# Turning the rounded tokens for the gate and up products by DMA transposes instead of TensorE and ScalarE, in a one-core vision-transformer layer

## The reference

```python
def _act_fake_quant(x, clip_factor):
    scale = jax.nn.sigmoid(clip_factor) * jnp.max(jnp.abs(x)) / QMAX
    return jnp.clip(_ste_round(x / scale), -QMAX - 1.0, QMAX) * scale

xq = _act_fake_quant(x, clip_x[0])                                # (32, 256, 256)
gate = jnp.einsum('bsh,ih->bsi', xq, _weight_fake_quant(w_gate))  # 704 columns
up = jnp.einsum('bsh,ih->bsi', xq, _weight_fake_quant(w_up))
h = _act_fake_quant(jax.nn.silu(gate) * up, clip_down[0])
return jnp.einsum('bsi,hi->bsh', h, _weight_fake_quant(w_down))
```

## Time and profile before

| | us |
|---|---|
| median of 3 runs | 961.52 (961.47 to 961.72) |
| the profiled execution, its own time | 966.27 |
| span in its trace | 964.5 |
| middle stage, first matmul of group 0 to last matmul of group 15 | 790.5 to 885.2 |
| TensorE, VectorE, ScalarE, GpSimd busy in the whole span | 831.7, 735.9, 632.9, 519.8 |

### The profile page before, as it was taken

The page is one execution under the profiler, slowest core; times in us unless marked ns, Lnnn a source line. Parts: engine busy times, 40 slices in busy tenths (PEclk is TensorE's granted clock), DMA queues, the critical chain, the costliest instruction groups (busy, mean ns, idle before and its releaser), DMA issues.

```text
span 964.5 us, 26048 instructions
## 1 busy us (share of the span) xinstructions
PE 831.7 (86%) x9061; PEld 490.0 (51%) x9070; DVE 735.9 (76%) x1309; ACT 632.9 (66%) x988; POOL 519.8 (54%) x545
## 2 busy tenths in 40 slices
PE   3788999999999999999999999999998859997775
PEld 2445555555555555555555555555554434443443
DVE  5845777777777777777777777777776659999898
ACT  3246666666666766666666666766766549996664
POOL 1345666566556656666666656556654327774000
PEclk8679999999999999999999999999999779999899
DMA  7000111111111111111111111111100000001488
GB/s 264 29 1 2 39 41 41 54 52 47 38 38 38 38 38 38 38 38 38 38 38 38 51 47 55 38 38 38 39 13 12 13 22 1 0 0 41 143 262 251
DMA packets 33158, 50.41 MB, mean 52 GB/s; under 512 B 2016, under 2 KB 28384, under 8 KB 33120
## 3 DMA queue, kind: packets, MB, share of 16 engines
q1 hardware_dynamic: 33120, 49.91, 16.4%
HBM read 33.13 MB, written 16.78 MB: 52 GB/s over the span
## 4 chain that ended last, share of the span: by engine, by line
PE 55%; DVE 26%; issue 10%; ACT 4%; POOL 1%; DVEq 1%; DMA 1%; ACTq 0%; SPq 0%; POOLq 0%
PE pair L439 10%; DVE act_all L1240 9%; PE pair L464 7%; PE pair L510 6%; PE pair L517 5%; PE pair L548 5%; PE pair L583 5%; PE pair L729 4%; DVE act_all L1281 4%; PE pair L494 3%; PE pair L532 3%; PE pair L552 2%; ACT ffn L986 2%; PE pair L572 2%; DVE ffn L1504 2%
## 5 line engine op out<-in xcount | busy, mean ns | idle before, releaser
L1240 DVE TENSOR_REDUCE act_all<-pair 128x8 f32<-128x1024 f32 x192 | 235.2, 1225 | 101.8 <-PE pair L517 101.1
L869 ACT ACTIVATE act_all<-pair 128x768 f32<-128x768 f32 x256 | 207.9, 812 | 135.0 <-PE pair L534 135.0
L1030 POOL TENSOR_SCALAR_AFFINE_SELECT act_all<-act_all 128x512 f32<-128x512 f32 x256 | 162.7, 641 | 101.9 <-ACT act_all L869 101.9
L1073 POOL TENSOR_TENSOR act_all<-act_all 128x2 f32<-128x2 f32 x64 | 60.9, 951 | 213.9 <-DVE act_all L1273 143.4
L439 PE MATMUL pair<-act_all 128*128 128x256 f16 (+1 forms) x960 | 120.7, 281 | 9.3 <-DVE act_all L1175 9.3
L861 ACT ACTIVATE act_all<-pair 128x1024 f16<-128x1024 f16 x64 | 65.7, 1027 | 79.2 <-PE pair L494 79.2
L439 PEld LDWEIGHTS pair<-act_all 128*128 128x128 f16 (+1 forms) x960 | 92.6, 100 | 28.1 <-issue 15.7
L510 PE MATMUL pair<-act_all,eye_b 128*128 128x512 bf16 x256 | 79.2, 392 | 26.5 <-DVE act_all L1240 25.9
L548 PE MATMUL pair<-act_all 128*32 128x256 f32 x1024 | 83.6, 399 | 1.3 <-POOL act_all L1030 1.2
L1068 POOL TENSOR_TENSOR act_all<-act_all 128x1280 f16<-128x1280 f32 x31 | 80.9, 2611 | 1.3 <-ACT act_all L799 1.3
L517 PEld LDWEIGHTS pair<-act_all 32*128 32x128 f16 x1536 | 43.9, 94 | 68.2 <-issue 66.9
(11 more groups left out here) (136 smaller groups left out, 1685.2 us busy)
## 6 DMA issues: line engine op xcount, KB each, us to landing
act_all<-x_t SPq DMA_DIRECT2D x32, 640.0 KB, 4.0
out<-act_all SPq DMA_DIRECT2D x32, 256.0 KB, 2.2
ffn<-out SPq DMA_DIRECT2D x16, 512.0 KB, 4.7
out<-ffn SPq DMA_DIRECT2D x16, 512.0 KB, 3.2
act_all<-w_down SPq DMA_DIRECT2D x1, 704.0 KB, 8.7
act_all<-w_emb SPq DMA_DIRECT2D x1, 640.0 KB, 3.9
ffn<-w_gate SPq DMA_DIRECT2D x1, 640.0 KB, 7.0
ffn<-w_up SPq DMA_DIRECT2D x1, 640.0 KB, 7.8
```

Of the source, the lines that this page charges most:

```text
L869: act.activation(probs[:, o:o + 2, 0:3, :].rearrange("p h k s -> p h (k s)"), pair[1][:, :].rearrange("p (h c) -> p h c", h=2)[:, :, 0:3 * P],
L1030: pool.affine_select(out=p, in_=p, pattern=[[0, 4], [1, P]], compare_op=ALU.is_ge, fill=0.0, base=0, channel_multiplier=-1).then_inc(maske ...
L1240: dve.tensor_reduce(to.rearrange("p (g k) -> p k g", g=GROUPS)[:, first:first + 2, :], pair[2][:, :].rearrange("p (k g t) -> p k g t", k=2 ...
```

## The change

The transposes leave TensorE, and their copies leave ScalarE. SyncE issues one transposing DMA for each group, from `xq[k]` to `xq_t[k]`, both in SBUF, 128 x 1024 bf16, on its queue. `xq_t` is laid out by tile of tokens, then by half of the 256 values, and the matmuls read their 512 columns as four runs of 128. The transfer of group `g` is issued once the group is widened (`xq_ready`) and all up matmuls of group g - 2, which read the same buffer, are done (`up_done`). TensorE waits for the arrival (`xq_turned[k]`, 16 for each transfer) before a group's first matmul, and GpSimd before it widens group g + 2 into the same `xq[k]`. SyncE waits for the last arrivals ahead of the last stage. TensorE's and ScalarE's loops now take in the last two groups.

```diff
+            def turn_x(g, k):
+
+                if g == 0:
+                    sp.wait_ge(xq_first_ready, 1)
+                else:
+                    sp.wait_ge(xq_ready, g)
+                if g >= 2:
+                    sp.wait_ge(up_done, (g - 1) * IM)
+                sp.dma_start_transpose(xq_t[k].rearrange("p b c t -> p (b c) t"),
+                                       xq[k].rearrange("p t e -> p (t e)")).then_inc(xq_turned[k], 16)
+
+            for g in range(NG):
+                turn_x(g, g % 2)
+            for k in range(2):
+                sp.wait_ge(xq_turned[k], 8 * NG)
+
             sp.wait_ge(act_ready, len(DVE_M) * NG)
             sp.wait_ge(act_by_pool, len(POOL_M) * NG)
-            sp.wait_ge(xq_t_ready, NG)
...
-                for c in range(DC):
-                    for t in range(GTT):
-                        o = (c * GTT + t) * 64
-                        mm = pe.transpose(bank[k][:, o:o + 64].bitcast(BF16), xq[k][:, t, c * P:(c + 1) * P],
-                                          eye_b[:, :])
-                mm.then_inc(xq_turned, 1)
-
-            def gate_up(g, k, ahead=True):
-                pe.wait_ge(xq_t_ready, g + 1)
+            def gate_up(half, k):
+                g = 2 * half + k
+                pe.wait_ge(xq_turned[k], 16 * half + 16)
                 xs = xq_t[k]
...
-                                mm = pe.matmul(b[:, :], w[:, c, m * P:(m + 1) * P], xs[:, c, :],
+                                mm = pe.matmul(b[:, :], w[:, c, m * P:(m + 1) * P], xs[:, :, c, :],
                                                start=(c == 0), stop=(c == DC - 1))
...
-                    if m == 3 and ahead:
-                        turn_x(g + 1, 1 - k)
-
-            turn_x(0, 0)
...
-                act.activation(xq_t[k].rearrange("p c t -> p (c t)"), bank[k][:, :].bitcast(BF16),
-                               ACT.Copy).then_inc(xq_t_ready, 1)
...
-                    if m == 3 and ahead:
-                        turned(g + 1, 1 - k)
...
                 if g >= 2:
-                    pool.wait_ge(xq_turned, g - 1)
+                    pool.wait_ge(xq_turned[k], 16 * (g // 2))
```

More of the change, by code:

```diff
@@ L224, in vit_layer @@
               for k in range(2)]
-        xq_t = [ffn[:, 1536 + 512 * k:2048 + 512 * k].bitcast(BF16).rearrange("p (c t) -> p c t", c=DC)
+        xq_t = [ffn[:, 1536 + 512 * k:2048 + 512 * k].bitcast(BF16).rearrange("p (b c t) -> p b c t", b=GTT, c=DC)
                 for k in range(2)]
@@ L300, in vit_layer @@
         xq_ready = sem("xq_ready")
-        xq_turned = sem("xq_turned")
-        xq_t_ready = sem("xq_t_ready")
+        xq_turned = [sem("xq_turned0"), sem("xq_turned1")]
         gate_done = sem("gate_done")
@@ L728, in gate_up @@
                             for c in range(DC):
-                                mm = pe.matmul(b[:, :], w[:, c, m * P:(m + 1) * P], xs[:, c, :],
+                                mm = pe.matmul(b[:, :], w[:, c, m * P:(m + 1) * P], xs[:, :, c, :],
                                                start=(c == 0), stop=(c == DC - 1))
                         else:
-                            for half in range(2):
+                            for half_ in range(2):
                                 for c in range(DC):
-                                    mm = pe.matmul(b[IH * half:IH * (half + 1), 0:GT // 2], w[:, c, m * P:I],
-                                                   xs[:, c, half * (GT // 2):(half + 1) * (GT // 2)],
+                                    mm = pe.matmul(b[IH * half_:IH * (half_ + 1), 0:GT // 2], w[:, c, m * P:I],
+                                                   xs[:, half_ * (GTT // 2):(half_ + 1) * (GTT // 2), c, :],
                                                    start=(c == 0), stop=(c == DC - 1))
                         mm.then_inc(signal, 1)
-                    if m == 3 and ahead:
-                        turn_x(g + 1, 1 - k)
-            turn_x(0, 0)
             pe.wait_ge(weights_ready, 2)
             gate_up(0, 0)
[L745 to L750, removed]
+            gate_up(0, 1)
+            with pe.Fori(1, NG // 2) as i:
+                gate_up(i, 0)
+                gate_up(i, 1)
             pe.wait_ge(act_ready, len(DVE_M) * NG)
@@ L967, in copy_up, with pass_b @@
                                ).then_inc(up_copied, 1)
[L969 to L973, removed]
-                act.activation(xq_t[k].rearrange("p c t -> p (c t)"), bank[k][:, :].bitcast(BF16),
-                               ACT.Copy).then_inc(xq_t_ready, 1)
-            def pass_b(half, k, ahead=True):
+            def pass_b(half, k):
                 g = 2 * half + k
@@ L989, in pass_b @@
                         copy_up(g, m)
-                    if m == 3 and ahead:
-                        turned(g + 1, 1 - k)
             widen_first()
-            turned(0, 0)
             act.wait_ge(x_scale_ready, 1)
@@ L997, in _ @@
             pass_b(0, 1)
-            with act.Fori(1, NG // 2 - 1) as i:
+            with act.Fori(1, NG // 2) as i:
                 pass_b(i, 0)
                 pass_b(i, 1)
-            pass_b(NG // 2 - 1, 0)
-            pass_b(NG // 2 - 1, 1, ahead=False)
             def widen(g, k):
```

## The result

The changed kernel takes 954.42 us (median of 4 runs, 953.13 to 954.62) against 961.5 of the kernel before: a ratio of 0.9917, interval 0.9890 to 0.9944, so 7.1 us faster where +1.6 was forecast. It lies outside the range of 959.8 to 1004. Later, 10 more runs of the same changed kernel gave 954.97 and a ratio of 0.9933 (0.9912 to 0.9954); 10 more of the kernel before gave 960.32, so the gain is 5.4 us between these two and 7.1 between the first.

The account below looks back on a forecast made before the run. The prediction took VectorE's own work, 5.74 us a group, to bound the middle stage. It summed +3.2 + 0.8 - 0.4 - 2.0 = +1.6 us on 961.5, giving 963.1 us, with a range of 959.8 to 1004.

Parts of the forecast that it names:

- Bound now: Middle stage: VectorE's own work, 5.74 us of a 5.88 us turn per group, sets the pace.
- Relief: Middle stage, work off TensorE and ScalarE: -2.0 us over groups 2 to 15, -0.4 us in VectorE's first full turn.
- VectorE's gap: Middle stage, idle time ahead of VectorE's product of piece 2: 0.14 us a group, the most that relief could give.
- T: Each group's transposing transfer, from its wait being met to arrival at the waiting engine: 5.3 us, bounds 2.2 and 17.6.
- Estimate (a): Transfer time from 64 pieces of 256 bytes per DMA engine at 52 ns each: 4.7 us.
- Estimate (b): Transfer time if SyncE makes it as 8 blocks, each at an issue time of 0.42 us: 5.3 us.
- Hidden or not: Middle stage after the start: the 5.3 us transfer fits narrowly into 5.7 us of room, and VectorE stays the bound.
- The rival formula (T + 5.8) / 2: Turn of a group if the transfer outlasts 5.7 us of room and TensorE starves; slower rival, chance 0.42.
- Start: Group 0 of the middle stage: +3.2 us waiting for the transfer, +0.8 us for first matmuls at the low clock.
- Last stage: Stage after the middle one: no term in the forecast's sum, so 0.
- The faster rival: Relief outweighs the start if the transfer takes under 2.6 us and the clock is no colder: 959.2 us, chance 0.08.

Follow-up runs that it names:

- ScalarE dummy: The changed kernel plus one unused ScalarE copy of 128 x 1024 elements behind the silu of piece 3 of each group; 963.99 us, ratio to before 1.0025.
- TensorE dummy: The changed kernel plus 8 transposes of weight blocks into an unused PSUM bank on TensorE behind piece 3 of each group; 956.65 us, ratio to before 0.9947.
- run in quarters: The changed kernel with each group's transfer issued as 4 transposes of 128 x 256; 965.46 us, ratio 1.0054.
- the eight blocks: The changed kernel with each group's transfer issued as 8 transposes of one 128 x 128 block; 1037.52 us, ratio 1.0761.
- the warming matmuls: Changed kernel, group 0 by TensorE and ScalarE, with 8 constant matmuls around group 0's transposes: 950.94 us; 9 more ahead of the last stage: 949.22 us.

## Why the prediction was wrong

- **Bound now.** Wrong, and this is the step that failed: "VectorE's own work is therefore 5.88 - 0.14 = 5.74 us a group, and it is the bound; the most that relief of the others can give is 0.14 us a group". VectorE's own work is 5.42. The ring of ScalarE and GpSimd set 5.88, and VectorE's stop was 0.46: 0.19 inside a merged row, and more ahead of piece 2 than durations show. The earlier trace rows held the hint: two products of 512 columns took 1.41 there, and one of 256 with one of 512 took 1.33, hardly less for three quarters of the columns. The earlier trace rows held it too: 19.32 of 20 us is not full.
- **Relief.** Forecast -2.4 in all, measured -7.5 (15 x 0.46 and 0.6 in the fill). The part of it that I had traced, silu 4 behind L974 and GpSimd behind that, was the right mechanism; I priced it by VectorE's gap and not by the ring it closes. The ScalarE dummy undoes the gain, the TensorE dummy doesn't. This, and not T, moved the forecast out of its range: with T = 3.4 and the rest as forecast the sum is 961.5 + 1.34 + 0.8 - 0.4 - 2.0 = 961.2.
- **T.** 5.3 forecast, 3.4 measured, inside the bounds of 2.2 and 17.6. Estimate (a) charged 52 ns for a piece of 256 bytes; from 785 to 870 us of the changed kernel 15846 packets took 25% of 16 engines, 21 ns each. Estimate (b) charged an issue for each block; one instruction of 1.23 us covers all eight.
- **Hidden or not.** Right: TensorE waits for a DMA once, at group 0. The rival formula (T + 5.8) / 2 was right in form; run in quarters, its constant is 5.3. It lacked the limit of SyncE's own issuing, which the eight blocks hit.
- **Start.** Forecast +3.2 for the wait and +0.8 for the clock, measured +1.25 and +1.1 (+1.35 and +0.5 in the second profile). T accounts for the wait's difference. The low clock was there: thirteen matmuls recorded from 785.8 to 790.9, at a granted 0.51.
- **Last stage.** 0 forecast, -0.85 measured between two profiles. That it belongs to the change is not shown: six of seven other versions with DMA transposes have 7.39 to 8.10 for the first 48 matmuls, like the kernel before. Why the low clock lasts for different times there was not tested; the warming matmuls show only that the clock is what that time hangs on.
- **The faster rival** had the right sign with a chance of 0.08, and put its condition wrongly at T under 2.6.

## What to carry to other kernels

Three engines busy for 93 to 97% of the time can all be waiting: a ring through shared buffers then sets the pace, and the engine that looks fullest has gaps inside merged rows. Add up a ring from an instruction round to its own next start, and look for every ring that the instruction stands in, before pricing its removal by somebody's gap. Put the work into one DMA instruction when an issue costs the same for a small as for a large transfer, and fill TensorE's idle time ahead of a dense stage.

## What was unexpected of the hardware

- A transposing DMA costs SyncE 1.23 to 1.27 us an issue, for 128 x 128, 128 x 256 and 128 x 1024 bf16 alike; a plain one 0.42. They land 2.3, 2.3 and 3.1 us after issue. The Trainium skill ("VectorE: DVE Perf Modes", the three transpose paths) has 1309 ns for a 128 x 128 block by DMA; this is near the issue here, and is not paid for each block of a larger transfer. The Trainium skill ("Advanced Engine Details and Errata", X-Bar Transpose) says that such transfers are as fast as plain ones; here neither the landing (3.1 against a store's 2.2 for 256 KB) nor the issue bears that out.
- Matmuls on constants in the gaps bring the clock to 1.00 for the first matmuls of group 0. They take 1.4 us off the middle stage (97.45 to 96.08) and 1.5 off the last one (73.00 to 71.49); the medians fall by 2.1 and 1.7.
